# A decoder layer with routed experts: the scales of the expert weights made in pieces, the first routing round spread over two steps

## What is computed

```python
x = layernorm(x + self_attention(x))                 # 16 heads of 16, an ALiBi bias
x = layernorm(x + cross_attention(context, x))       # 16 heads of 16, a mask on the context
x = layernorm(x + experts(x))
def experts(x):                                      # 4096 tokens, 8 experts, F = 1024
    probs = softmax(x @ gate_w.T)                    # 4096 x 8
    topk_probs, topk_idx = top_k(probs, 2)
    hidden = relu(x @ w1[e] + b1[e])
    all_out = hidden @ w2[e] + b2[e]
    return sum(topk_probs * all_out[topk_idx])
```

## Time and profile before

| | us |
|---|---|
| median of 3 runs | 1312.58 |
| lowest and highest run | 1311.31, 1317.23 |
| the profiled execution | 1317.72 |
| its span | 1315.8 |
| TensorE busy | 1088.9 (83%) |
| VectorE busy | 976.3 (74%) |
| ScalarE busy | 567.6 (43%) |
| GpSimd busy | 489.3 (37%) |

### The profile page before, as it was taken

How to read it: one execution, slowest core, us unless ns; L and a number is a source line. 1 busy time by engine, 2 the same in 40 slices (tenths; PEclk the granted TensorE clock), 3 DMA queues, 4 the chain that set the end, 5 groups by cost and what they waited for, 6 DMA issues and landing times. The chain is left out here.

```text
span 1315.8 us, 32466 instructions
## 1 busy us (share of the span) xinstructions
PE 1088.9 (83%) x9894; PEld 773.2 (59%) x9895; DVE 976.3 (74%) x2213; ACT 567.6 (43%) x1025; POOL 489.3 (37%) x603
## 2 busy tenths in 40 slices
PE   3778989999888889989998661889999999999970
PEld 2445666666665566656665441667777777777750
DVE  1568888888887888888887663577777777777754
ACT  1434555555554566666665420223222323232325
POOL 1233343334433435545552574022322322322224
PEclk7889999999999899999998865899999999999995
DMA  8577866686648488879886676652222222222228
GB/s 179 136 179 162 193 141 180 175 206 135 164 96 188 114 234 240 196 218 262 240 207 196 205 244 234 247 166 45 40 44 43 43 43 42 42 44 40 45 30 259
DMA packets 153666, 193.98 MB, mean 147 GB/s; under 512 B 30636, under 2 KB 133948, under 8 KB 149323
## 3 DMA queue, kind: packets, MB, share of 16 engines
q1 hardware_dynamic: 139144, 174.67, 49.8%
q0 software_dynamic: 13296, 17.83, 8.1%
q10 hardware_dynamic: 1152, 0.53, 0.2%
HBM read 122.63 MB, written 66.16 MB: 143 GB/s over the span
## 5 line engine op out<-in xcount | busy, mean ns | idle before, releaser
L1397 PE MATMUL HB<-xhi,W 128*128 128x128 f16 x2272 | 292.0, 221 | 21.6 <-issue 16.6
L1397 PEld LDWEIGHTS HB<-xhi,W 128*128 x2272 | 202.0, 98 | 66.1 <-issue 48.1
L1602 POOL DMA_INDIRECT d_sums<-ysc,tok x71 | 111.0, 1563 | 322.3 <-ACT ysc L1463 208.5
L1397 PE MATMUL HB<-xlo,W 128*128 128x128 f16 x1136 | 225.0, 220 | 0.0
L836 DVE TENSOR_REDUCE peaks<-SA 128x4 f32<-128x1024 f32 x128 | 156.6, 1223 | 65.9 <-PE SA L688 65.4
L1113 ACT ACTIVATE PT<-SB 128x1024 f32<-128x1024 f32 x128 | 131.1, 1024 | 130.9 <-PE SB L736 128.9
L1397 PEld LDWEIGHTS HB<-xlo,W 128*128 x1136 | 111.9, 98 | 49.7
L1519 DVE SCALAR_TENSOR_TENSOR hlo<-HB,hhi 128x512 f16<-128x512 f32 x142 | 98.2, 692 | 55.4 <-ACT hhi L1455 51.6
L1455 ACT ACTIVATE hhi<-HB 128x512 f16<-128x512 f32 x142 | 84.2, 593 | 119.7 <-DVE HB L1511 119.5
L1463 ACT ACTIVATE ysc<-yb,wv 128x256 f32<-128x256 f32 x71 | 36.1, 508 | 192.0 <-DVE yb L1543 183.9
L1511 DVE SCALAR_TENSOR_TENSOR HB<-HB,SC,b1c 128x512 f32<-128x512 f32 x142 | 107.1, 754 | 13.9 <-PE HB L1397 7.9
(11 more groups left out here) (205 smaller groups left out, 2375.0 us busy)
## 6 DMA issues: line engine op xcount, KB each, us to landing
wst<-in_w SPq DMA_DIRECT2D x32, 1024.0 KB, 10.1
d_w<-w SPq DMA_DIRECT2D x16, 1024.0 KB, 8.2
W<-d_w SPq DMA_DIRECT2D x16, 1024.0 KB, 7.2
k_stack<-d_k SPq DMA_DIRECT2D x96, 128.0 KB
XB<-d_rows SPq DMA_DIRECT2D x65, 130.0 KB
d_q<-q_part SPq DMA_DIRECT2D x16, 384.0 KB, 6.0
d_k<-k_part SPq DMA_DIRECT2D x16, 384.0 KB, 2.7
q_stack<-d_q SPq DMA_DIRECT2D x16, 384.0 KB, 4.5
```

Of the source, the lines that this page charges most:

```text
L1397: mm = pe.matmul(out, w.rearrange("p e n -> p (e n)"), x[n % 2][:, k, :], start=(k == 0 and half == 0 and x is xhi), stop=(k == KT - 1 and ...
L1602: pool.indirect_dma_start(YS, bass.IndirectOffsetOnAxis(ap=tok[n % 6][:, 0:1], axis=0), ysc[n % 2][:, :], None, compute_op=ALU.add).then_i ...
```

## The change

The reduction over the partitions moves behind the splits of q and cq in GpSimd's step 8. The scales are made in three pieces, ahead of turns 5, 6 and 7 of step 8, in place of one ahead of turn 3; the last piece sets the semaphore that ScalarE waits for in step 9. `choose` is cut in two, `nominate` (three instructions) and `elect` (two, and two more for k = 0). Round 0 has centre, shares, nominate(0) and elect(0) in step 9 (behind turns 0, 2, 4 and 6) and nominate(1), elect(1), join and place in step 10 (behind turns 0, 2, 4 and 6), with the counting products and the O product's wait in step 10 too. Step 10 is written out, and the loop runs over steps 11 to 13. The scatters of round 0 are issued at five a step in steps 11 to 15, and three at the start of step 16. The arithmetic is the same.

```diff
--- before.py
+++ after.py
@@ -168,11 +168,18 @@
         chain(dve.tensor_tensor(self.pr, self.ex, self.bc(rden), ALU.mult))
 
     def choose(self, dve, chain, k):
-        w, best = self.meta(k), self.small(3)
+        self.nominate(dve, chain, k)
+        self.elect(dve, chain, k)
+
+    def nominate(self, dve, chain, k):
+        w = self.meta(k)
         chain(dve.tensor_reduce(w, self.pr, AX.X, ALU.max))
         chain(dve.tensor_tensor(self.eq, self.pr, self.bc(w), ALU.is_equal))
         chain(dve.tensor_tensor(self.eq, self.eq, self.rt["desc"][:, :].unsqueeze(1)
                                 .to_broadcast([P, self.n, NE]), ALU.mult))
+
+    def elect(self, dve, chain, k):
+        best = self.small(3)
         chain(dve.tensor_reduce(best, self.eq, AX.X, ALU.max))
         chain(dve.tensor_tensor(self.oh[:, k], self.eq, self.bc(best), ALU.is_equal))
         if k == 0:
@@ -381,7 +388,8 @@
         step(7, "max")
         step(8, "scale")
         step(9, "halve")
-        looped(step, eng, 10, B - 2, "halve", chain, per)
+        step(10, "halve")
+        looped(step, eng, 11, B - 2, "halve", chain, per)
         step(B - 2, "halve")
         step(B - 1, "halve")
         step(B, "halve")
@@ -421,9 +429,9 @@
 
     router = [Router(rt, n, sem, BK[1][:, 0:2 * P], BK[1][:, 2 * P:4 * P]) for n in range(4)]
     ROUTE_EXPS = {(9, 1): 0, (B, 0): 1, (B + 1, 1): 2, (B + 1, 7): 3}
-    ROUTE_COUNTS = {(9, 6): (0, "V", 10), (B, 3): (1, "Oc", B - 2), (B + 1, 3): (2, "Oc", B - 1),
+    ROUTE_COUNTS = {(10, 6): (0, "V", 11), (B, 3): (1, "Oc", B - 2), (B + 1, 3): (2, "Oc", B - 1),
                     (B + 1, 7): (3, "R", B - 1)}
-    ROUTE_READ = {("O", 9): 1, ("R", B): 2, ("R", B + 1): 3}
+    ROUTE_READ = {("O", 10): 1, ("R", B): 2, ("R", B + 1): 3}
 
     def at_route(u, i, where):
         return isinstance(i, int) and (i, u) in where
@@ -962,10 +970,14 @@
             chain(dve.tensor_copy(wp[:, 0:2], wg[:, 0:2]))
             chain(dve.tensor_scalar(wp[:, 2:3], wg[:, 0:1], float(D), wg[:, 2:3], ALU.mult, ALU.add))
             chain(dve.tensor_scalar(wp[:, 0:3], wp[:, 0:3], 2.0 ** -100, 2.0 ** 100, ALU.max, ALU.min))
+
+        def powers():
             bits = wp[:, 0:3].bitcast(I32)
             chain(dve.tensor_scalar(bits, bits, 0x7F800000, None, ALU.bitwise_and))
             chain(dve.reciprocal(wp[:, 3:6], wp[:, 0:3]))
             chain(dve.tensor_scalar(SC[:, 0:2], wp[:, 3:5], 2.0 ** 13, None, ALU.mult))
+
+        def products():
             chain(dve.tensor_scalar(SC[:, 2:3], wp[:, 5:6], 2.0 ** 14, None, ALU.mult))
             chain(dve.tensor_scalar(SC[:, 3:4], SC[:, 2:3], wp[:, 0:1], 2.0 ** -13, ALU.mult, ALU.mult))
             chain(dve.tensor_scalar(SC[:, 4:5], wp[:, 1:2], wp[:, 2:3], 2.0 ** -27, ALU.mult, ALU.mult))
@@ -978,11 +990,16 @@
                     router[0].centre(dve, chain)
                 elif u == 2:
                     router[0].shares(dve, chain)
-                elif u == 3:
-                    router[0].choose(dve, chain, 0)
                 elif u == 4:
-                    router[0].choose(dve, chain, 1)
-                elif u == 5:
+                    router[0].nominate(dve, chain, 0)
+                elif u == 6:
+                    router[0].elect(dve, chain, 0)
+            elif i == 10:
+                if u == 0:
+                    router[0].nominate(dve, chain, 1)
+                elif u == 2:
+                    router[0].elect(dve, chain, 1)
+                elif u == 4:
                     router[0].join(dve, chain)
                 elif u == 6:
                     router[0].place(dve, chain)
@@ -1019,8 +1036,12 @@
             for u in range(2 * NG):
                 if mode == "scale" and u == 0:
                     greatest()
-                if mode == "scale" and u == 3:
+                if mode == "scale" and u == 5:
                     scales()
+                if mode == "scale" and u == 6:
+                    powers()
+                if mode == "scale" and u == 7:
+                    products()
                 if u < NG:
                     top(u, 0, i)
                     spread_and_divide(u, i)
@@ -1203,14 +1224,14 @@
             pool.tensor_tensor(shift[:, :], shift[:, :], minus[:, 0:QT], ALU.mult).then_inc(sem(f"rstd{c}"), 1)
 
         def step(i, mode):
+            if i == B:
+                send_rows(pool, sem, rt, XS, 0, 25, 3)
+            split("q", i + 1)
+            split("cq", i - 1)
             if mode == "scale":
                 pool.wait_ge(sem("wm"), 1)
                 pool.partition_all_reduce(wg[:, :], wm[:, :], P, bass.bass_isa.ReduceOp.max
                                           ).then_inc(sem("wg"), 1)
-            if i == B:
-                send_rows(pool, sem, rt, XS, 0, 24, 4)
-            split("q", i + 1)
-            split("cq", i - 1)
             if not (isinstance(i, int) and i < 0):
                 split("k", i + 1)
             deviations("c", i - 2)
@@ -1231,8 +1252,8 @@
                                    ).then_inc(sem("xbo"), 1)
             if i == 2:
                 route_constants()
-            if 10 <= i < B:
-                send_rows(pool, sem, rt, XS, 0, 4 * (i - 10), 4)
+            if 11 <= i < B:
+                send_rows(pool, sem, rt, XS, 0, 5 * (i - 11), 5)
             elif i == B:
                 send_rows(pool, sem, rt, XS, 1, 0, 24)
             elif i == B + 1:
```

## The result

The median of 20 runs fell from 1312.78 us (1305.33 to 1319.66) to **1309.37 us** (1304.04 to 1313.10). The ratio is 0.9967, its 95% interval 0.9953 to 0.9981: 2.5 to 6.2 us faster, and within the 0.5% that the prediction counted as no change. It lies inside the predicted range and 2.2 us above the forecast.

The account below looks back on a forecast made before the run. The prediction took TensorE's chain as the bound, delayed by VectorE's scales and routing blocks in steps 8 and 9. It summed 2.5 us from step 8 and 2.9 from routing, 5.4 less: 1307.2 us, range 1303.4 to 1311.6.

Parts of the forecast that it names:

- What bounds the kernel: Steps 7 to 10: TensorE's own chain bounds; VectorE's scales and choose(0) make it wait; reachable excess 6.4 and 7.1 us.
- Routing: Steps 9 and 10: spreading the first routing round leaves 4.25 us of excess against 7.1, so 2.9 us less.
- Nominate(0): Step 9, behind turn 4: no slack there, so 0.95 us of its 1.14 falls on the path.
- counting and placing: Step 10, a step later than before: 0.98 us of wait plus about 0.7 for three small groups, 1.7 in all.
- Scatters: Steps 11 to 16: a fifth scatter a step is covered by GpSimd's wait for the moments, 1.1 us to spare; cost 0.
- Step 8: Moved reduction and split scales: 2.2 us of TensorE delay plus 1.7 for one clock fall, 3.9 against 6.4, 2.5 less.
- the k path: Step 8 into 9: k's parts ready 6.5 us later, partly lost in SP's wait, partly covered by step 8's lengthening; cost 0.
- the sign of its own error: Start of step 9: a wait of the first scores on k_stack would make the forecast wrong; no size given.
- rival B: Waits merely move: k path or uncovered routing eats the gain; 1.2 to 2.9 us less, about 1310.5; chance 0.17.
- Rival C: Step 8: reduction holds GpSimd longer in its new place; doubled to 27.4 us, the kernel takes 1319.5 us; chance 0.04.
- Rival D: Step 8: k split starts at once behind the reduction, without the trailing 7.3 us; 8.1 less, 1304.5 us; chance 0.07.
- Rival A: No clock fall in step 8: 7.1 less, 1305.5 us; with step 12's fall gone too, 1303.8; chance 0.35 with that addition.

Follow-up runs that it names:

- the two halves by themselves: Two kernels: routing spread but reduction and scales as in the kernel before, ratio 0.9990; reduction and scales moved but routing as in the kernel before, ratio 0.9981.
- without the hold: Changed kernel with a plain GpSimd copy in place of the all-reduce, so scales differ by partition; ratio to the kernel before 0.9971.
- the first execution: Profiled execution of the changed kernel in its original measurement against the kernel before; median 1309.37 us, ratio 0.9967.
- the third: Profiled execution of the changed kernel, unaltered, in its second repetition, on a slower chip; ratio to the kernel before 1.0015.
- the second: Profiled execution of the changed kernel, unaltered, in its first repetition, on a slower chip; ratio to the kernel before 0.9962.

## Why the prediction was right, and where it was not

**What bounds the kernel** held: both blocks on VectorE were what TensorE waited for, as the two halves by themselves showed.

**Routing**, 4.25 us of new excess forecast. Nominate(0) cost 0.66 (the wait rose from 0.42 to 1.08 us) for 0.95, elect(0) 0.74 for 1.0, join 0.2 (0.63 against 0.42) for 0.6, counting and placing 1.5 for 1.7; nominate(1) and elect(1) cost nothing, as taken. That is 3.1. The sign of every term was right; nominate(0) and elect(0) cost TensorE 0.6 of their own length (0.66 of 1.14, 0.74 of 1.15), join a third of what was taken.

**Scatters**, 0: right on the chip of the result, with 0.9 us to spare where 1.1 was worked out. On the slower chips the steps that hold them are longer than before, as shown above, and there the term is open.

**Step 8.** The hold (13.57 for 13.7), the end of the cq split (15.37 us behind the step's first scores for 15.25) and the k split's place (28.94 for 28.9) were right. ScalarE stood 2.50 us on the shift for 3.0, TensorE 1.27 on avs for 2.1. VectorE's pieces delayed TensorE by 0.37 in turn 5 (0.79 for 0.42), not by 1.2 to 2.8; the second piece ran under the wait on avs, as the prediction said. The clock didn't fall in step 8 in any of the three executions. So its excess without the k path was 1.84 (44.68 - 42.84) for 3.9.

**The step that failed is the k path, costed at 0.** The k split was late, SP's k reads began 4.7 us later in the step than without the hold (36.7 us against 32.0 behind its start), and TensorE stood up to 2.01 us for k_stack ahead of the first scores of step 9, with a fall of the clock behind it: 3.7 us in the first execution, 3.5 or more in the third, nearly nothing in the second. The prediction had named this wait as the sign of its own error, and it is the first half of its rival B, which gave the whole 1310.5 us; the measured 1309.37 lies nearer to that than to the forecast. The forecast of the three steps stood because this miss of 3.7 and the 2.1 too much in step 8 and 1.1 too much in routing nearly cancel: 137.26 against a forecast 136.95. That is luck. By the prediction's own cut each step by itself comes within 0.7 us of its forecast, 46.84 for 46.6, 45.64 for about 45 and 44.78 for 45.4, and for the same reason: the k_stack wait of 2.01 fills the place of a fall that did not come in step 8, and that fall the place of the routing that was cheaper in step 9. By that cut step 8's excess is 4.0 for 3.9, from other causes than those that were summed.

**Rival C**, the hold doubled, did not come; in its new place the hold is 13.1 to 13.8 us in all six executions that have it there. **Rival D**, no trailing part, is excluded by the 7.61 us. **Rival A**, no fall in step 8, came true for step 8, but the fall stood in step 9 instead.

That the whole moved by 3.4 us and the three steps by 4.8 is within the interval (2.5 to 6.2). On the two slower chips the ratio of the changed kernel was 0.9962 and 1.0015, with intervals that hold both 1 and 0.9967; whether the gain is the same there isn't settled, and steps 11 to 14 speak for a smaller one.

## What to carry to other kernels

Before moving a long hold on an engine, list what is queued behind it in the new place and follow each item to its last reader through the queues, DMAs included: a late producer that was harmless behind another wait turns into the next wait once that one is gone. Short instructions on a busy engine are not free in the holes of its timeline; a hole counts as slack only if what stands behind it isn't what the bounding engine waits for next. Before pricing tiny VectorE instructions, look at what GpSimd runs beside them: the same ten took 4.7 us beside its splits and 1.9 beside its silence. And where single steps gain a few us, compare the steps over several executions: falls of the clock of 1.6 us each change their step with the waits, and the same kernel gave 136.18, 137.26 and 139.70 us for the same three steps.

## What the runs showed of the hardware

An all-reduce over partitions on GpSimd whose row is 0.4 to 0.6 us long holds the engine for 13.1 to 13.8 us in ten executions, with 5.58 to 5.95 us of silence ahead of the row; a second one right behind adds nothing (13.51). In the two kernels that have it behind xbo the silence ahead is 7.4 to 7.5 us, and the next instruction, which waits for VectorE's moments, starts 14.8 to 14.9 us after xbo's end.

A VectorE tensor_scalar on two or three elements a partition took 0.33 to 1.21 us beside GpSimd's splits, each ending within 0.03 us of GpSimd's instruction, and 0.17 us beside an idle GpSimd; on one element a partition it took 0.15 to 0.22 either way.

The clock can fall behind waits of 0.73 us (four executions, at the start of step 10, one of which had fallen in step 8 as well) and keep up behind the same wait of 0.73 or 0.74 (five executions, the first and third of the changed kernel among them, which had a fall in step 8 or 9). All fourteen executions have at least one fall in steps 8 to 10, the one without the long waits and without the hold too; what decides in which step stays open.

Steps 3 to 7, where the clock doesn't fall, repeat within 0.05 us over chips on which the whole kernel differs by 2%.
